# A two-layer image kernel: the remainder's parts of the two output products on separate row halves of the array

## The chip, the cores and the metric

The kernel runs on one core of one Trainium2 chip. A core has TensorE (matmuls; PE in the profile, its weight loads PEld), VectorE (DVE), ScalarE (ACT), GpSimd (POOL) and SyncE (SP, which here only issues DMAs), each with an instruction stream of its own. They meet through semaphores. The metric is the device time of one execution in microseconds (us), lower is better.

## The reference

For a batch of 8 images, x of 192 channels by 64x64 pixels, two layers follow each other:

```
xn  = layernorm over channels(x);  xz = in_proj (384x192) . xn;  xc, z = halves of xz
xc  = silu(conv3x3 depthwise(xc) + b)
y   = sum of four selective scans over 4096 pixels (rows, columns, both directions)
y   = layernorm over channels(y) * out_norm_w + out_norm_b      # LN
y   = y * silu(z)                                               # gate
x1  = x + out_proj (192x192) . y                                # the mix product
theta, phi, g = 96x192 products of x1;  f = softmax(theta^T phi) over 4096 pixels
out = x1 + W (192x96) . (g f^T) + b
```

The 192 channels do not fit the 128 partitions: a tensor over channels is held as a tile of 128 channels and a remainder of 64.

## The kernel before

A loop over the 8 images has three stages, with a barrier of all engines between them. First `project` and the four scans; then the mix stage, which this case is about; then the attention. The 4096 pixels go in 8 chunks (NCH) of 512 (T). Nothing reorders instructions: each engine's stream stands in the order in which its block is written, and waits on semaphores with hand-counted values.

The mix stage is written as `run_mix(eng, step)`: `step(-1, "n")`, `step(0, "np")`, a hardware loop over pairs of steps for chunks 1 to 4, then steps 5 and 6 with "np" and step 7 with "p". In step c, "n" normalizes chunk c+1 and "p" takes chunk c through the products. One step is, by engine (lines of the profile):

- PE: the mean of chunk c+1 (L400, L401 over `pad0` and `yt`), the mix product of chunk c (L629, L630), the variance of chunk c+1 (L400, L401 over `sqa`, `sqb`), two products for the running maximum of attention ("tops", L616), phi (L642, L643), g (L650, L651), two more tops (L616).
- DVE: subtract the mean (`deviate`, L1150, L1151), prepare the remainder of a later chunk (`yt`, L1298), add x to the mix product (`na` L1324, `nb` L1325), two maxima (L1309), then for chunk c+1 four operations: scale `da`, `db` by 1/std (L1335, L1336), shift and gate them into `oa` and `ob` (L1340, L1343); then the low halves `phl`, `gtl` (L1348, L1352), two more maxima (L1309) and a small maximum `mx` (L1359).
- ACT: squares of `da` and `db` (L783, L784), logarithm and exponential for 1/std (L789, L791), copies and splits (L968 to L977).

The variance matmul waits for the squares, they for the deviations, the scaling for 1/std; the mix product waits for `oa` and `ob` (`gated_ready`) and DVE's `na` for the mix product (`mixed`).

In the mix product `wo0` holds the weights for the first 128 input channels and `wo1` those for the remaining 64 in its rows 0 to 63, zeros in rows 64 to 127. Output bank 2 of PSUM takes the first 128 output channels, bank 3 a 128-wide slice whose first 64 rows are the remainder's outputs. `ob` holds the remainder of the input in rows 0 to 63; its rows 64 to 127 are zeroed by GpSimd at the start of each mix stage (`zero_rows`, L1034), so both remainder matmuls run over 128 rows. Tiles alias others in memory, which is why the zeros are set anew for every image. One matmul of these float32 tiles is two records in the trace.

Of the kernel before, what the change touches and what calls it, by code (L numbers as in the profile page):

```python
# [21 lines left out]
ALU = mybir.AluOpType  # L22
# [3 lines left out]
B, C, HH, WW = 8, 192, 64, 64  # L26
L = HH * WW
P = 128
R = C - P
# [21 lines left out]
V_LNW, V_LNB, V_CB, V_DS, V_ONW, V_ONB, V_WB = 0, 2, 4, 6, 14, 16, 18  # L51
# [3 lines left out]
def build(nc, nb, x, vec, w_in, w_x, w_dt, sel, fold, ident, w_out, w_att, gb, w_w, out):  # L55
# [3 lines left out]
    with ctx:  # L59
        def sb(name, shape, dt=F32, where=ctx):  # L60
            return where.enter_context(nc.sbuf_tensor(name, shape, dt))
# [24 lines left out]
        gate = sb("gate", [P, 2, L])  # L86
# [8 lines left out]
        vecs = sb("vecs", [P, NV])  # L95
# [16 lines left out]
        wo1 = sb("wo1", [P, C])  # L112
# [31 lines left out]
        db = sb("db", [R, T], where=lnx)  # L144
        sqa = sb("sqa", [P, T], where=lnx)
        sqb = sb("sqb", [P, T], where=lnx)
# [3 lines left out]
        nb_ = sb("nb", [P, T], where=lnx)  # L150
        oa = sb("oa", [P, T], where=lnx)
        ob = sb("ob", [P, T], where=lnx)
        yt = sb("yt", [P, 2, T], where=lnx)
# [21 lines left out]
        ps = ctx.enter_context(nc.psum_tensor("ps", [P, 8, T], F32))  # L175
# [10 lines left out]
        def barrier(eng, b, n):  # L186
# [6 lines left out]
        S = {n: sem(n) for n in (  # L193

            "pads_set", "rows_zero", "row_one", "xb_zero", "bias_row", "consts_set", "dsum_set", "borders_set", "scan_set", "att_set", "thc_set", "mx_link",

            "x_loaded0", "x_loaded1", "x_free", "mean_ready", "dev_ready", "sq_ready", "var_ready", "rstd_ready",

            "norm_ready", "z_ready", "xc_ready", "zs_ready", "gate_ready", "tap_ready",
            "conv_link", "conv_ready", "tapw_ready", "rem_ready", "rem_free", "cs_ready", "u_ready",  # L200

# [11 lines left out]
        block = ctx.enter_context(nc.Block())  # L213
        LOADS = [(vecs[:, :], vec), (foldw[:, R:P], fold), (eye[:, :], ident), (wo0[:, R:C], w_out[0:P, 0:P]), (wo0[:, 0:R], w_out[0:P, P:C]),
                 (wo1[0:R, R:C], w_out[P:C, 0:P]), (wo1[0:R, 0:R], w_out[P:C, P:C]),
                 (wa0[:, :], w_att[0:P]), (wa1[0:R, :], w_att[P:C]), (wa1[R:R + 1, 2 * O:3 * O], gb), (ww[:, :], w_w), (wdt[0:NX + 1, :].rearrange("p (k n) -> p k n", n=2 * P)[:, 0::2, :], w_dt.rearrange("p (k n) -> p k n", n=2 * P)[:, 0::2, :])]
        wk = w_x.rearrange("p (k n) -> p k n", n=64)
        for w, rows_ in ((wx0, slice(0, P)), (wx1, slice(P, 2 * P))):
            for s, k in enumerate((0, 2)):
                at = s * P  # L220
                LOADS += [(w[:, at:at + NX], w_x[rows_, 64 * k:64 * k + NX]), (w[:, at + R + RANK + NS:at + R + NX], w_x[rows_, 64 * k + RANK + NS:64 * k + NX])]
                for i, kk in enumerate((1, 3)):
                    c_of, m = w_x[rows_, 64 * kk + RANK + NS:64 * kk + NX], at + NX + NS * i
# [168 lines left out]
        def _(pe):  # L392
            mm = pe.matmul
# [23 lines left out]
            with pe.Fori(0, nb) as b:  # L417
# [201 lines left out]
                def step(c, par, which):  # L619
                    i, j = b * NCH + c, b * NCH + (c + 1)  # L620
                    n = (b * 2 + 1) * NCH + (c + 1)
                    q = 1 - par
                    if "n" in which:
                        pe.wait_ge(S["yt_ready"], j + 1)
                        mean_of(0, pad0[:, bass.ds((c + 1) * T, T)], yt[:, q, :], "mean_ready")
                    if "p" in which:
                        pe.wait_ge(S["gated_ready"], i * 2 + 4)
                        for bank, lo, hi in ((2, R, C), (3, 0, P)):
                            mm(ps[:, bank, :], wo0[:, lo:hi], oa[:, :], start=True, stop=False)  # L629
                            m = mm(ps[:, bank, :], wo1[:, lo:hi], ob[:, :], start=False, stop=True)  # L630
                        m.then_inc(S["mixed"], 1)
                    if "n" in which:
                        pe.wait_ge(S["sq_ready"], n * 2 + 2)
                        mean_of(1, sqa[:, :], sqb[:, :], "var_ready")
                    early = "p" in which and not (isinstance(c, int) and c == 0)
                    if early:
                        early_top(c, 0)
                        early_top(c, 1)
                    if "p" in which:
                        pe.wait_ge(S["x1_ready"], i * 2 + 2)  # L640
                        pe.wait_ge(S["phl_ready"], i + 1)
                        mm(ps[:, 4, :], wa0[:, O:O + P], na[:, :], start=True, stop=False)  # L642
                        mm(ps[:, 4, :], wa1[:, O:O + P], nb_[:, :], start=False, stop=True)\  # L643
                            .then_inc(S["phi_ready"], 1)
                        if not early:
                            theta_of(na[:, :], nb_[0:R, :])
                        pe.wait_ge(S["gtl_ready"], i + 1)
                        for t in range(T // P):
                            dst = ps[:, 5, t * P:t * P + O]
                            mm(dst, na[:, t * P:(t + 1) * P], wa0[:, 2 * O:3 * O], start=True, stop=False)  # L650
                            m = mm(dst, nb_[:, t * P:(t + 1) * P], wa1[:, 2 * O:3 * O], start=False, stop=True)  # L651
                        m.then_inc(S["gt_ready"], 1)
                    if early:
                        early_top(c, 2)
                        early_top(c, 3)
                pe.wait_ge(S["rows_zero"], b * 4 + 6)
                pe.wait_ge(S["row_one"], b + 2)
                run_mix(pe, step)
                barrier(pe, b, 1)
# [363 lines left out]
        def _(pool):  # L1023
# [8 lines left out]
            def zero_rows(n, one, tiles):  # L1032
                for t in tiles:
                    pool.memset(t, 0.0).then_inc(S["rows_zero"], 1)  # L1034
                pool.wait_ge(S["rows_zero"], n)
                pool.sem_inc(mark, 1)
                pool.memset(nb_[R:R + 1, :], 1.0).then_inc(S["row_one"], 1)
                pool.wait_ge(S["row_one"], one)
                pool.sem_inc(mark, 1)

            zero_rows(2, 1, (sqb[R:P, :], nb_[R:P, :]))
            with pool.Fori(0, nb) as b:
# [14 lines left out]
                for r, t in enumerate(padi):  # L1057
                    for edge in (t[:, 0:1, :], t[:, PW - 1:PW, :], t[:, 1:PW - 1, 0:1], t[:, 1:PW - 1, PW - 1 - r:PW]):
                        m = pool.memset(edge, 0.0)  # L1059
# [42 lines left out]
                barrier(pool, b, 0)  # L1102


                zero_rows(b * 4 + 6, b + 2, (yt[R:P, :, :], sqb[R:P, :], nb_[R:P, :], ob[R:P, :]))
                pool.memset(xb[R:P, :, :], 0.0).then_inc(S["xb_zero"], 1)
                pool.wait_ge(S["xb_zero"], b + 2)
                pool.sem_inc(mark, 1)
# [9 lines left out]
        def _(dve):  # L1118
            TT, TS, STT = dve.tensor_tensor, dve.tensor_scalar, dve.scalar_tensor_tensor
# [12 lines left out]
            TS(win0[:, :], win0[:, :], vecs[:, V_LNW:V_LNW + 1], None, ALU.mult)  # L1132
            TS(win1[0:R, :], win1[0:R, :], vecs[0:R, V_LNW + 1:V_LNW + 2], None, ALU.mult)

            for name, n in (("x_free", 2), ("fin_ready", 2), ("gated_ready", 2), ("norm_ready", 2), ("gate_ready", 1), ("tap_ready", 1), ("rem_free", 1), ("u_ready", 1),
                            ("xlo_ready", 1), ("dt_ready", 1), ("hc_ready", 3), ("cbc_ready", 4), ("summed", 3), ("y0_added", 1),
                            ("y1_added", 1), ("rows_saved", 16), ("scan_link", 6), ("dbu_ready", 4), ("du_ready", 2), ("dtpre_ready", 1), ("phl_ready", 1), ("gtl_ready", 1),
                            ("top_read", 2), ("pf_ready", 2), ("yraw_ready", 1), ("shift_loaded", 64), ("pv_ready", 2), ("pl_ready", 2),
                            ("yn_ready", 1), ("out_stored", 32)):
                dve.sem_inc(S[name], n)  # L1140
# [25 lines left out]
            with dve.Fori(0, nb) as b:  # L1166
# [144 lines left out]
                def step(c, par, which):  # L1311
                    i, j = b * NCH + c, b * NCH + (c + 1)
                    n = (b * 2 + 1) * NCH + (c + 1)
                    if "n" in which:
                        dve.wait_ge(S["gated_ready"], j * 2 + 2)
                        deviate(n, pad0[:, bass.ds((c + 1) * T, T)], yt[0:R, 1 - par, :])
                        if not isinstance(c, int) or c + 2 < NCH:
                            add_rem(c + 2, par)
# [13 lines left out]
                    if "n" in which:  # L1332
                        dve.wait_ge(S["rstd_ready"], n * 2 + 2)
                        at = j * 2
                        STT(da[:, :], da[:, :], vecs[:, V_ONW:V_ONW + 1], rstd[:, :], ALU.mult, ALU.mult).then_inc(S["mix_link"], 1)  # L1335
                        STT(db[:, :], db[:, :], vecs[0:R, V_ONW + 1:V_ONW + 2], rstd[0:R, :], ALU.mult, ALU.mult)\  # L1336
                            .then_inc(S["mix_link"], 1)
                        sl = bass.ds((c + 1) * T, T)
                        dve.wait_ge(S["mix_link"], at + 1)
                        STT(oa[:, :], da[:, :], vecs[:, V_ONB:V_ONB + 1], gate[:, 0, sl], ALU.add, ALU.mult)\  # L1340
                            .then_inc(S["gated_ready"], 1)
                        dve.wait_ge(S["mix_link"], at + 2)
                        STT(ob[0:R, :], db[:, :], vecs[0:R, V_ONB + 1:V_ONB + 2], gate[0:R, 1, sl], ALU.add, ALU.mult)\  # L1343
                            .then_inc(S["gated_ready"], 1)
                    if "p" in which:
                        sl = bass.ds(c * T, T)
                        dve.wait_ge(S["phh_ready"], i + 1)
# [169 lines left out]
```

## Time and profile before

| | |
|---|---|
| median of 3 runs | 9318.6 us (9313.8 to 9319.06) |
| profiled execution | 9313.63 us, span 9311.9 us |
| PE busy | 8651.9 us, 93% |
| DVE busy | 7376.5 us, 79% |
| ACT busy | 6095.7 us, 65% |
| POOL busy | 3281.4 us, 35% |
| mix product matmuls (L629, L630) | 64 executions of 4 matmuls, 256 records of each line |
| `ob` operation (L1343) | 64 executions, median 736 ns |

Busy time on PE is modelled where matmuls overlap, so a step that shows PE fully busy need not be one that PE sets. A row of the timeline gives start, duration, engine, line, tiles and, in brackets, the idle time of that engine before it and what ended it.

### The profile page before, as it was taken

The page shows a single profiled execution, that of the slowest core. Times are in us where ns is not written, and L with a number is a line of the kernel's source. Part 1 is how long each engine was busy: PE and PEld are TensorE (multiplying, and loading weights), DVE is VectorE, ACT ScalarE, POOL GpSimd, SP SyncE. Part 2 cuts the span into 40 slices and gives each one's busy share as a digit, 9 for nine tenths or more (in the row PEclk, how much of TensorE's full clock was granted, in tenths as well). Part 3 has the DMA queues.
Part 4 walks back from the last instruction along what each step waited for, and adds up shares of the span by engine and source line. Part 5 has one row for each costly group of instructions (what it writes and reads, how often), then busy time and mean ns, then how long its engine had stood idle before and what let it go on. Part 6 is the DMA issues. An engine that isn't in the chain of part 4 may idle for free. (4 is left out here: it accounts for less than half of the span.)

```text
span 9311.9 us, 104022 instructions
## 1 busy us (share of the span) xinstructions
PE 8651.9 (93%) x26448; PEld 4648.7 (50%) x26448; DVE 7376.5 (79%) x8229; ACT 6095.7 (65%) x7440; POOL 3281.4 (35%) x1853
## 2 busy tenths in 40 slices
PE   7899988999989999899988999889998899988999
PEld 2336743367433674336743367333673336733376
DVE  6987769877798777987779876798767987689876
ACT  6765677656776567755677556775567755677566
POOL 2860028600286002860038500385003850038400
PEclk9999999999999999999999999999999999999999
DMA  1320013200132001320023200232002320023200
GB/s 53 111 86 13 10 49 115 82 13 10 56 111 81 11 11 56 115 76 11 11 62 111 76 10 10 66 114 69 10 12 67 111 69 10 12 68 117 65 9 12
DMA packets 286693, 503.21 MB, mean 54 GB/s; under 512 B 142155, under 2 KB 143215, under 8 KB 253431
## 3 DMA queue, kind: packets, MB, share of 16 engines
q1 hardware_dynamic: 286199, 497.81, 17.6%
q8 instruction: 166, 2.72, 0.1%
q14 instruction: 328, 2.69, 0.1%
HBM read 467.99 MB, written 29.47 MB: 53 GB/s over the span
## 5 line engine op out<-in xcount | busy, mean ns | idle before, releaser
L1387 DVE TENSOR_TENSOR pl<-pf,ph 128x1024 fp32r<-128x1024 f32 x1024 | 1254.6, 1225 | 1016.6 <-ACT ph L1013 1008.7
L1241 DVE TENSOR_TENSOR_SCAN h<-ps,h,dbu 128x512 f32<-128x512 f32 x1536 | 1883.8, 1267 | 55.4 <-POOL dbu L1080 30.0
L1080 POOL TENSOR_TENSOR dbu<-bs,du 128x1024 f32<-128x1024 f32 x768 | 1809.3, 2371 | 54.1 <-POOL du L1071 54.1
L1013 ACT ACTIVATE ph<-pf 128x1024 fp32r<-128x1024 f32 x1024 | 1085.3, 1060 | 748.0 <-PE ps L701 747.8
L877 ACT ACTIVATE ps<-dt,negA 128x512 f32<-128x512 f32 x1536 | 1037.9, 687 | 701.8 <-DVE h L1241 701.8
L1007 ACT ACTIVATE pf<-ps 128x1024 f32<-128x1024 f32 x1024 | 1051.4, 1027 | 537.4 <-PE ps L688 537.4
L1371 DVE TENSOR_REDUCE mx<-ps 128x1 f32<-128x512 f32 x1792 | 1168.9, 683 | 77.1 <-PE ps L606 61.9
L1059 POOL MEMSET pad<- 128x66 f32 (+1 forms) x64 | 7.2, 202 | 3179.4 <-DVE fa L1416 3179.2
L1249 DVE TENSOR_TENSOR hc<-h,ps 128x1024 f32<-128x1024 f32 x768 | 937.9, 1221 | 108.0 <-PE ps L487 16.6
L487 PE MATMUL ps<-xhl,selr 128*128 128x512 f32 x1536 | 761.2, 581 | 246.4 <-DVE hc L1249 246.2
L1065 POOL TENSOR_TENSOR dt<-dt,ze 128x1024 f32<-128x1024 f32 x256 | 604.6, 2362 | 1057.7 <-ACT dt L870 1057.1
L686 PE MATMUL ps<-thc,phh 97*128 97x512 f32 x2048 | 847.7, 414 | 6.8 <-ACT thc L990 6.8
L1071 POOL TENSOR_TENSOR du<-dt,u 128x512 f32<-128x512 f32 x512 | 712.7, 1413 | 317.0 <-DVE dt L1231 316.4
L699 PE MATMUL ps<-ph,gth 128*97 128x512 f32 x2048 | 817.7, 399 | 5.5 <-ACT yraw L995 5.5
L687 PE MATMUL ps<-thc,phl 97*128 97x512 f32 x2048 | 816.9, 399 | 0.0
L688 PE MATMUL ps<-thc,phh 97*128 97x512 f32 x2048 | 813.6, 397 | 0.0
L701 PE MATMUL ps<-pl,gth 128*97 128x512 f32 x2048 | 806.8, 394 | 0.0
L700 PE MATMUL ps<-ph,gtl 128*97 128x512 f32 x2048 | 806.4, 394 | 0.0
L487 PEld LDWEIGHTS ps<-xhl,selr 128*128 128x128 f32 x1536 | 245.0, 191 | 905.0 <-DVE hc L1249 732.4
L606 PE MATMUL ps<-phh,thc 96*128 96x512 f32 x1824 | 632.5, 408 | 41.8 <-DVEq L189 18.8
L528 PE MATMUL ps<-hc,eye 128*128 128x512 f32 x1024 | 483.9, 594 | 0.0
L686 PEld LDWEIGHTS ps<-thc,phh 97*128 97x128 f32 x2048 | 389.9, 190 | 174.0 <-issue 78.9
(202 smaller groups left out, 14511.0 us busy)
## 6 DMA issues: line engine op xcount, KB each, us to landing
bs<-rows SPq DMA_DIRECT2D x256, 1024.0 KB, 5.1
bs<-rows SPq DMA_DIRECT2D x512, 256.0 KB, 6.1
xa<-in_x SPq DMA_DIRECT2D x130, 256.0 KB, 2.9
xb<-in_x SPq DMA_DIRECT2D x130, 128.0 KB, 3.0
out<-fa SPq DMA_DIRECT2D x64, 256.0 KB, 2.1
rdb<-rden SPq DMA_DIRECT2D x56, 192.0 KB, 3.4
out<-fa SPq DMA_DIRECT2D x64, 128.0 KB, 2.4
xhl<-ct SPq DMA_DIRECT2D x256, 8.0 KB
```

The lines of the kernel that those rows point to most:

```text
L487: m = mm(flat(ps[:, 4 + e, :]), selr[:, j * P:(j + 1) * P], src, start=True, stop=True)
L686: mm(dst, kk, thc[par][0][:, :], start=True, stop=False)
L687: mm(dst, phl[:, m * P:(m + 1) * P], thc[par][0][:, :], start=False, stop=False)
L699: mm(dst, gth[:, m, :], ph[:, mp % 2, e, :], start=(m == 0), stop=False)
L877: A(ps[:, 2 + e, :], dt[par][:, 0 if j < NS else 1, :], ACT.Exp, scale=negA[:, k * NT + j:k * NT + j + 1]).then_inc(S["dA_ready"], 1)
L1007: A(pf[:, mp % 2, :, :], ps[:, 2 * (mp % 2):2 * (mp % 2) + 2, :], ACT.Exp)\
L1013: A(ph[:, mp % 2, :, :], pf[:, mp % 2, :, :], ACT.Copy).then_inc(S["ph_ready"], 1)
L1080: pool.tensor_tensor(dbu[:, q, :, :], bs[par][:, q, :, :], du[:, r:r + 1, :].to_broadcast([P, 2, T]), ALU.mult).then_inc(S["dbu_ready"], 1)
L1241: dve.tensor_tensor_scan(h[:, j, ::step], ps[:, 2 + e, ::step], dbu[:, q, e, ::step], h[:, j, end:end + 1], ALU.mult, ALU.add)\
L1249: TT(hc[:, q, :, :], h[:, 2 * q:2 * q + 2, :], ps[:, 4:6, :], ALU.mult).then_inc(S["hc_ready"], 1)
L1371: dve.tensor_reduce(mx[:, t, m:m + 1], ps[:, 5 + j % 2, :], AX.X, ALU.max)\
L1387: TT(pl[:, mp % 2, :, :], pf[:, mp % 2, :, :], ph[:, mp % 2, :, :].bitcast(F32), ALU.subtract)\
```

## The change

`wo1` gets a second copy of its weights in rows 64 to 127. DVE computes the gated remainder twice, into rows 0 to 63 and into rows 64 to 127 of `ob`, so `gated_ready` counts three per chunk where it counted two. PE issues the two 128-row matmuls first (banks 2 and 3), then the two remainder matmuls, each over 64 rows: bank 2 from rows 0 to 63 and bank 3 from rows 64 to 127. GpSimd no longer zeroes rows 64 to 127 of `ob`. SyncE loads two more pieces of weights at the start of the program.

```diff
                  (wo1[0:R, R:C], w_out[P:C, 0:P]), (wo1[0:R, 0:R], w_out[P:C, P:C]),
+                 (wo1[R:P, R:C], w_out[P:C, 0:P]), (wo1[R:P, 0:R], w_out[P:C, P:C]),
...
                     if "p" in which:
-                        pe.wait_ge(S["gated_ready"], i * 2 + 4)
-                        for bank, lo, hi in ((2, R, C), (3, 0, P)):
+                        pe.wait_ge(S["gated_ready"], i * 3 + 6)
+                        halves = ((2, R, C, slice(0, R)), (3, 0, P, slice(R, P)))
+                        for bank, lo, hi, _ in halves:
                             mm(ps[:, bank, :], wo0[:, lo:hi], oa[:, :], start=True, stop=False)
-                            m = mm(ps[:, bank, :], wo1[:, lo:hi], ob[:, :], start=False, stop=True)
+                        for bank, lo, hi, at in halves:
+                            m = mm(ps[:, bank, :], wo1[at, lo:hi], ob[at, :], start=False, stop=True)
                         m.then_inc(S["mixed"], 1)
...
-                pe.wait_ge(S["rows_zero"], b * 4 + 6)
+                pe.wait_ge(S["rows_zero"], b * 3 + 5)
...
-                zero_rows(b * 4 + 6, b + 2, (yt[R:P, :, :], sqb[R:P, :], nb_[R:P, :], ob[R:P, :]))
+                zero_rows(b * 3 + 5, b + 2, (yt[R:P, :, :], sqb[R:P, :], nb_[R:P, :]))
...
-                        dve.wait_ge(S["gated_ready"], j * 2 + 2)
+                        dve.wait_ge(S["gated_ready"], j * 3 + 3)
...
-                        STT(ob[0:R, :], db[:, :], vecs[0:R, V_ONB + 1:V_ONB + 2], gate[0:R, 1, sl], ALU.add, ALU.mult)\
-                            .then_inc(S["gated_ready"], 1)
+                        for r in range(2):
+                            STT(ob[r * R:r * R + R, :], db[:, :], vecs[0:R, V_ONB + 1:V_ONB + 2], gate[0:R, 1, sl], ALU.add, ALU.mult)\
+                                .then_inc(S["gated_ready"], 1)
```

On DVE, the second step of the loop before, from the wait for 1/std (L1333) to `gtl`:

```order
L1333 ISA
L1335 SCALAR_TENSOR_TENSOR da<-da,vecs,rstd 128x512
L1336 SCALAR_TENSOR_TENSOR db<-db,vecs,rstd 64x512
L1339 REGISTER_ALU
L1340 REGISTER_ALU
L1340 SCALAR_TENSOR_TENSOR oa<-da,vecs,gate 128x512
L1343 ISA
L1343 SCALAR_TENSOR_TENSOR ob<-db,vecs,gate 64x512
L1348 ISA
L1348 TENSOR_TENSOR phl<-phf,phh 96x512
L1352 ISA
L1352 TENSOR_TENSOR gtl<-ps,gth 128x4x96
```

The same stretch now (line numbers are shifted by three or four):

```order
L1338 SCALAR_TENSOR_TENSOR da<-da,vecs,rstd 128x512
L1339 SCALAR_TENSOR_TENSOR db<-db,vecs,rstd 64x512
L1342 ISA
L1343 REGISTER_ALU
L1343 SCALAR_TENSOR_TENSOR oa<-da,vecs,gate 128x512
L1345 REGISTER_ALU
L1347 ISA
L1347 SCALAR_TENSOR_TENSOR ob<-db,vecs,gate 64x512 x2
L1352 ISA
L1352 TENSOR_TENSOR phl<-phf,phh 96x512
L1356 ISA
L1356 TENSOR_TENSOR gtl<-ps,gth 128x4x96
```

The second `ob` operation stands between the first and `phl`, and with it everything that DVE does until the next `deviate` moves one operation back.

On PE, the same step before, from the mean of chunk c+1 to its variance:

```order
L400 MATMUL ps<-pad,avg 128x512
L401 MATMUL ps<-yt,avg 128x512
L627 ISA
L629 MATMUL ps<-oa,wo 128x512
L630 MATMUL ps<-ob,wo 128x512
L629 MATMUL ps<-oa,wo 128x512
L630 MATMUL ps<-ob,wo 128x512
L633 ISA
L400 MATMUL ps<-sqa,avg 128x512
```

And now:

```order
L401 MATMUL ps<-pad,avg 128x512
L402 MATMUL ps<-yt,avg 128x512
L628 ISA
L631 MATMUL ps<-oa,wo 128x512 x2
L633 MATMUL ps<-ob,wo 128x512 x2
L636 ISA
L401 MATMUL ps<-sqa,avg 128x512
```

The number of matmuls is unchanged. The two of the remainder now stand side by side, over different rows, directly ahead of the variance.

## Rows read from the trace of the kernel before

**Rows 1.** Windows, busy us by engine, granted clock: stage start, one loop step.
```profile
640.00:655.00 15.00, 10.52 (x13) 3.96 (x14) 5.30 (x8) 2.47 (x4) 8.58 (x6) 0.59 0.11 35
...
684.00:696.00 12.00, 11.79 (x43) 6.42 (x42) 10.01 (x16) 5.36 (x10) 0.00 (x0) 1.00 0.11 33
```

**Rows 2.** Timeline, one loop step: start, duration, engine, line, tiles, [idle before].
```profile
684.28 1.29 DVE L1309 TENSOR_REDUCE mx<-ps 128x1 f32<-128x512 f32 x2 [0.51 <-PE ps L616]
...
687.47 0.74 DVE L1343 SCALAR_TENSOR_TENSOR ob<-db,vecs,gate 64x512 f32<-64x512 f32 x1
...
688.13 0.68 DVE L1348 TENSOR_TENSOR phl<-phf,phh 96x512 f32 x1
...
690.01 1.02 PE L629 MATMUL ps<-oa,wo 128*128 128x512 f32 x2
...
690.55 0.17 DVE L1359 TENSOR_TENSOR mx<-mx 128x4 f32<-128x4 f32 x1
...
691.30 0.69 DVE L1150 TENSOR_TENSOR da<-pad,ps 128x512 f32<-128x512 f32 x1 [0.58 <-issue]
...
692.59 1.02 PE L630 MATMUL ps<-ob,wo 128*128 128x512 f32 x2
...
693.15 0.61 ACT L784 ACTIVATE sqb<-db 64x512 f32<-64x512 f32 x1
...
693.82 1.12 PE L400 MATMUL ps<-sqa,avg 128*128 128x512 f32 x2 [0.21 <-ACT sqb L784]
...
696.08 1.29 DVE L1309 TENSOR_REDUCE mx<-ps 128x1 f32<-128x512 f32 x2 [0.91 <-PE ps L616]
```

**Rows 3.** Timeline, the step after it.
```profile
702.68 0.69 DVE L1150 TENSOR_TENSOR da<-pad,ps 128x512 f32<-128x512 f32 x1 [0.17 <-issue]
...
704.53 0.61 ACT L784 ACTIVATE sqb<-db 64x512 f32<-64x512 f32 x1
...
705.23 1.09 PE L400 MATMUL ps<-sqa,avg 128*128 128x512 f32 x2
```

**Rows 4.** Timeline, start of the mix stage of the first image.
```profile
638.63 0.52 POOL L1034 MEMSET nb<- 64x512 f32 x1
639.10 0.52 POOL L1034 MEMSET ob<- 64x512 f32 x1
...
640.35 2.08 PE L400 MATMUL ps<-pad,avg 128*128 128x512 f32 x2 [3.89 <-POOL nb L1037]
```

**Rows 5.** Timeline, mix product of chunk 0 and variance of chunk 2.
```profile
654.67 1.12 PE L629 MATMUL ps<-oa,wo 128*128 128x512 f32 x2 [1.58 <-DVE ob L1343]
...
656.58 0.61 ACT L784 ACTIVATE sqb<-db 64x512 f32<-64x512 f32 x1
...
669.98 0.61 ACT L784 ACTIVATE sqb<-db 64x512 f32<-64x512 f32 x1
...
670.75 1.02 PE L400 MATMUL ps<-sqa,avg 128*128 128x512 f32 x2
```

**Rows 6.** Timeline, 64-row matmuls (64*96) between 128-row ones.
```profile
661.73 1.02 PE L598 MATMUL ps<-na,wa 128*96 128x512 f32 x2
...
662.68 1.10 PE L599 MATMUL ps<-nb,wa 64*96 64x512 f32 x2
...
663.71 0.46 PE L650 MATMUL ps<-wa,na 128*128 128x96 f32 x2
```

**Rows 7.** Timeline, variance of chunk 7 and mix product of chunk 7.
```profile
727.10 0.61 ACT L784 ACTIVATE sqb<-db 64x512 f32<-64x512 f32 x1
...
728.00 1.02 PE L400 MATMUL ps<-sqa,avg 128*128 128x512 f32 x2
...
734.23 1.13 PE L629 MATMUL ps<-oa,wo 128*128 128x512 f32 x2
...
737.96 0.69 DVE L1324 TENSOR_TENSOR na<-ps,xa 128x512 f32<-128x512 f32 x1 [1.32 <-PE ps L630]
```

**Rows 8.** Timeline, weight loads at the start of the program.
```profile
6.26 2.17 SPq L297 DMA_DIRECT2D wo<-in_w_out  x4
```

More of the change, by code:

```diff
@@ L1133, in _ @@
             TS(win1[0:R, :], win1[0:R, :], vecs[0:R, V_LNW + 1:V_LNW + 2], None, ALU.mult)
-            for name, n in (("x_free", 2), ("fin_ready", 2), ("gated_ready", 2), ("norm_ready", 2), ("gate_ready", 1), ("tap_ready", 1), ("rem_free", 1), ("u_ready", 1),
+            for name, n in (("x_free", 2), ("fin_ready", 2), ("gated_ready", 3), ("norm_ready", 2), ("gate_ready", 1), ("tap_ready", 1), ("rem_free", 1), ("u_ready", 1),
                             ("xlo_ready", 1), ("dt_ready", 1), ("hc_ready", 3), ("cbc_ready", 4), ("summed", 3), ("y0_added", 1),
```

## The prediction

> **What bounds the kernel now.** The page's busy shares come first: PE 93%, DVE 79%. They are averages over three stages and the change touches only the mix stage, so the windows come next. In one step of that stage PE is busy 11.79 of 12.00 us and DVE 10.01, at full clock [rows 1]. That reads like a PE bound. The timeline decides, because PE's busy time is modelled. The reader is to follow one step from variance to variance.
>
> PE starts a matmul of the mix product every 0.86 us (690.01 to 692.59 is three of them), so the four end their stream at 692.59 + 0.86 = 693.45. The variance matmul starts at 693.82, on the squares of `db`, which end at 693.15 + 0.61 = 693.76 [rows 2]. So PE waits 0.37 us, and the squares set the start. The squares follow `deviate`, 691.30 to variance being 2.52 us. `deviate` follows DVE's own stream: from the first maxima at 684.28 to `mx` at 690.55 DVE has no idle time (the row of `deviate` shows the first, 0.58 us of issue at the loop's edge, where the loop branches) [rows 2]. The first maxima wait for the tops, which stand on PE behind the variance: 693.82 to 696.08, 2.26 us. So there is a ring: variance, tops, DVE's stretch up to `deviate` (691.30 - 684.28 = 7.02 us at the loop's edge; 702.68 - 696.08 = 6.60 inside it), squares, variance. Inside the loop: 2.26 + 6.60 + 2.51 (702.68 to the squares' end at 704.53 + 0.61 = 705.14, plus the 0.06 us hand-over seen at 693.76 to 693.82, rounded together) = 11.37 us, against 705.23 - 693.82 = 11.41 measured [rows 2, 3]. The ring explains the period. In that step the mix product's stream is free at about the same time (PE's row at 705.23 shows no idle), so PE is second by 0.03 us, not far behind.
>
> **The change, part by part.** All times are for one image; the profiled execution has 8, and I sum against its 9313.63 us (span 9311.9 and 1.7 around it). The median of the runs is 5.0 us above that.
>
> DVE's second `ob`. Each 64x512 operation of this kind holds DVE from 687.47 to 688.13, 0.66 us [rows 2]. It comes after the scaling and ahead of `phl`, `gtl`, two maxima, `mx` and `deviate`, all of them in the ring. Nothing of that stretch waits, so nothing absorbs it. It issues 8 times per image, in steps -1 to 6. That the output now lies on rows 64 to 127 no row shows for this operation; I take the same 0.66.
>
> PE's mix product. Before, 4 x 0.86 = 3.44 us. Two matmuls on separate row halves could run side by side; no row of the trace has such a pair, so I bound the saving s. At best both remainder matmuls take the time of one: 0.86, less the change from 128-row to 64-row work. The rows for that are L598 to L599, 0.95 us where the stream gives 0.86, so 0.09, call it 0.10; and back, L599 to L650, 1.03, so 0.17 [rows 6]. Best case s = 0.76. At worst nothing overlaps and both switches are paid: s = -0.26. I take s = 0.33: each float32 matmul is two records, issued first-first-second-second, and if they start in order, only the second half of the one (0.43) can lie beside the first half of the other, less 0.10. That is between the ends, and is my choice.
>
> TensorE: Matmul & The Clock Gate (Part 3, the mechanism) in the Trainium skill says that matmuls in distinct row groups start about 4 ns apart, though in program order; taken for the whole pair it would give the best case, s = 0.76 less a hair, and the sum would be 2.2 us per image by the working below. TensorEngine Tiling (Key Properties) in the Trainium skill says against this that a change of tiling mode drains the engine; the trace agrees, with the 0.09 and 0.17 us just read.
>
> Where s counts. Inside the loop it counts nothing: the mix product's end is followed by the wait for the squares, which comes later than before. What was hidden behind 3.44 us of matmuls becomes PE idle time. It counts at the two edges, where the mix product itself is on the path.
>
> Now the shift of each point against before:
> - Stage start. PE's first mean waits for GpSimd's zeroing; one 64x512 memset fewer, 639.10 - 638.63 = 0.47 us [rows 4]: -0.47.
> - Mix product of chunk 0. It waits for `ob` (1.58 us idle), so its start moves by +0.66. The variance of chunk 1 follows in PE's stream (the squares end at 657.19, after +0.66 at 657.85; the stream, 654.67 + 3.44 + 0.33, at 658.44): +0.66 - 0.33 = +0.33 [rows 5].
> - Step 0. DVE's extra operation falls before the wait for `gth` and costs nothing. The variance of chunk 2 starts at 670.75 in PE's stream, its squares end at 670.59, 670.64 with hand-over: the 0.33 carried on loses 0.11: +0.22 in all [rows 5].
> - Steps 1 to 4, variances of chunks 3 to 6: +0.66 each by the ring, less the 0.03 by which the squares (705.14 + 0.06) were ahead of PE's stream (705.23) in the step of rows 3, taken for three of the four: 4 x 0.66 - 0.09 = +2.55. 1/std starts from the same variance, and DVE shows no wait for it, so it moves along [rows 2, 3].
> - Step 5, variance of chunk 7: squares ended at 727.71, PE's stream was free at 728.00. With hand-over 0.24 of slack: 0.66 - 0.24 = +0.42 [rows 7].
> - Step 6 and the mix product of chunk 7: it starts at 734.23, as `ob` ends (the row shows no idle, `ob` in the same place of the step takes its 0.74), and now waits for the second: +0.66. Its end releases `na` at 737.96: -0.33. Net +0.33 [rows 7].
> Sum: -0.47 + 0.33 - 0.11 + 2.55 + 0.42 + 0.33 = +3.05 us per image, 24.4 us for eight.
>
> The two weight loads. SyncE took 2.17 us to issue four pieces of `wo` [rows 8], 0.54 each, and every engine waits for the last load: +1.1 us, once.
>
> Total +25.5 us: 9313.6 + 25.5 = 9339 in the profile's terms, 9344 as a median. With s = 0.76 the edges give 0.43 less twice, 2.19 per image, +18.6 in all, 9337. With s = -0.26 the edges give 0.59 more twice, and the variance of chunk 2 is set by the later stream, 0.37 more in place of the squares: 4.6 per image, +38, 9357.
>
> The 64-row copy, the earlier `na` and `nb` in the loop, the register instructions and the semaphore counts I take as nothing: DVE waits for the tops after `nb` in any case (0.51 and 0.91 us [rows 2]), the register instructions lie beside 0.7 us operations. If they lay at the loop's edge, where DVE issues for 0.58 us, they could be worth 0.1 either way, three times an image: 2 us.
>
> **Rivals.**
> First, the PE bound. If the stream of PE and not the ring sets the period (for it: PE is 11.79 of 12.00 busy; the step of rows 3 has no idle before the variance), each np step loses s: 7 steps x 0.33 to 0.76 x 8 = 18 to 43 us, with -0.47 x 8 and +1.1: 9318.6 - 21 to - 45, about 9298 to 9274, faster. Against it: this needs DVE's 0.66 to vanish, and DVE has no idle time between the maxima and `mx`. Chance 7%.
>
> Second, DVE's idle time swallows the operation (0.51, 0.58 and the wait for the mix product in each step [rows 2]) and PE's saving ends in the wait: only the edges remain, -0.47 and at most -0.33 twice: about -9 + 1 us, 9311, no change. Against it: these idle times lie in the ring's other arcs or are issue time. Chance 9%.
>
> Third, the saving s is at its best or above (the pair fully beside each other and the switch hidden), 18.6 us and a little less with a shorter loop edge: 9335, just within what counts as no change. Same mechanism as the forecast, chance 14%.
>
> Fourth, the clock. PE's idle time ahead of the variance grows from 0.37 to about 0.37 + 0.33 + 0.66 = 1.4 us in each step. The granted clock was 0.59 in the stage's first 15 us, where PE had idled 3.89 us [rows 1, 4]; it was 1.00 in the step shown, with 0.37 idle. If the half level (1.2 GHz) lasted one step longer at the start, a step's mix and variance matmuls (6 x 0.86 us) would take 5 us more, of which DVE's ring hides part: 2 to 5 us per image, +16 to +40 more: 9360 to 9384. Against it: PE worked through the 1.58 us wait at 654.67 and ran at 0.86 us per matmul right after. Chance 7%.
>
> **How the numbers follow.** The ring with s between -0.26 and 0.7 has the remaining 63%; it is the likeliest and gives 9344. About 0.2%, 19 us, is what a measurement of this kernel can tell from no change. Slower by more than that: 63 + 7 + a little of the third = 71%. Within: the rest of the third, the second and the lower end of the forecast, 21%. Faster: 8%. The range holds the ring's ends and the third rival: 9331 to 9358; left out are the PE bound, the swallowed operation and the clock.
>
> **What would show it.** Right: the loop's steps take 12.0 us (12.4 at the edge) where they took 11.4 and 11.8; DVE runs gapless from maxima to `mx` with two `ob` rows 0.66 apart; PE shows 1.3 us or more of wait for `sqb` ahead of the variance in each step; the first mean of a stage starts 0.47 us earlier after the barrier. The start-to-start time from the first 128-row matmul of the mix product to the `mixed` release gives s. Wrong would be a step of 11.4 us or less, `deviate` waiting for the mean instead of DVE's stream, a variance matmul without a wait, or a granted clock below 1.00 in the loop's steps.

## The result, and the profile after

| | before | after |
|---|---|---|
| median | 9313.8 us (5 runs, 9305.2 to 9319.1) | 9362.2 us (5 runs, 9344.1 to 9365.7) |
| ratio after/before | | 1.0050, 95% interval 1.0035 to 1.0064 |
| profiled execution | span 9311.9 us, clock 0.978 | span 9342.3 us, clock 0.979 |

The change made the kernel slower, as forecast, but by 48 us in the medians where 25.5 was forecast. The median, 9362, lies 4 us above the range of 9331 to 9358. The profiled execution is 30.4 us longer in span. So there are two questions: whether the 30 us are the ones that were reasoned out, and what the other 18 are.

The timeline of the step of the changed kernel that answers [rows 2, 3] (start, duration, engine, line, tiles, idle before):

```profile
697.81 1.12 PE L401 MATMUL ps<-sqa,avg 128*128 128x512 f32 x2 [1.72 <-ACT sqb L787]
...
700.07 1.29 DVE L1312 TENSOR_REDUCE mx<-ps 128x1 f32<-128x512 f32 x2 [1.13 <-PE ps L617]
...
703.26 1.51 DVE L1347 SCALAR_TENSOR_TENSOR ob<-db,vecs,gate 64x512 f32<-64x512 f32 x2
...
704.80 0.69 DVE L1352 TENSOR_TENSOR phl<-phf,phh 96x512 f32 x1
...
705.79 1.88 PE L631 MATMUL ps<-oa,wo 128*128 128x512 f32 x4
...
707.52 0.69 DVE L1153 TENSOR_TENSOR da<-pad,ps 128x512 f32<-128x512 f32 x1 [0.17 <-issue]
707.60 1.13 PE L633 MATMUL ps<-ob,wo 64*128 64x512 f32 x4
708.13 0.67 DVE L1154 TENSOR_TENSOR db<-yt,ps 64x512 f32<-64x512 f32 x1
708.83 1.03 DVE L1301 TENSOR_TENSOR yt<-gate,ycol 64x512 f32 x1
...
710.03 1.12 PE L401 MATMUL ps<-sqa,avg 128*128 128x512 f32 x2 [1.30 <-ACT sqb L787]
```

From one variance matmul to the next is 12.22 us, against 11.41 in the step of [rows 2] and 11.37 in the one after it. PE now waits 1.30 us for the squares where it showed no wait; 1.72 at the loop's edge, where it showed 0.21. From 700.07 to 707.19 DVE is without idle time, as before. The two `ob` operations take 703.26 to 704.80, 0.77 each and not 0.66. The two 64-row matmuls run side by side as intended: four records of the 128-row product take 1.88 us, four of the 64-row product 1.13 (a record alone takes 0.59 or more), that is 0.75 saved, less 0.09 for the later start (705.79 + 4 x 0.43 = 707.51, against 707.60).

The two edges, answering to [rows 4, 5, 7]:

```profile
639.54 0.52 POOL L1037 MEMSET nb<- 64x512 f32 x1
...
640.79 2.07 PE L401 MATMUL ps<-pad,avg 128*128 128x512 f32 x2 [3.42 <-POOL nb L1040]
...
655.88 3.23 PE L631 MATMUL ps<-oa,wo 128*128 128x512 f32 x4 [2.12 <-DVE ob L1347]
...
741.18 1.98 PE L631 MATMUL ps<-oa,wo 128*128 128x512 f32 x4 [0.58 <-DVE ob L1347]
...
744.27 0.69 DVE L1327 TENSOR_TENSOR na<-ps,xa 128x512 f32<-128x512 f32 x1 [0.56 <-PE ps L633]
```

PE's idle time before the first mean fell from 3.89 to 3.42 us, by the memset's 0.47. The mix product of chunk 7 now waits for `ob` (0.58), and from its start to `na` it is 3.09 us, where it was 3.73: s = 0.64, not 0.33. At 655.88 the four records take 3.23 us in place of 1.88. By the trace's record of the granted clock, the half level at the stage's start had ended 2.8 us earlier. PE waited 2.12 us for the second `ob` (1.58 before), and 0.6 us into the product of chunk 0 the clock fell to its 1.2 GHz level again. Five of the eight images have such a product of chunk 0; in the profile before it is three.

The weight loads, answering to [rows 8]:

```profile
6.26 3.45 SPq L298 DMA_DIRECT2D wo<-in_w_out  x6
...
35.90 0.26 DVE L1124 TENSOR_SCALAR negA<-vecs 128x24 f32<-128x24 f32 x1 [35.90 <-DMA win<-in_w_in]
```

That first DVE operation stood at 34.59 before: +1.31 us.

The account of the 30.4 us, from start times of the mix products. Each part is taken from images with the same clock on both sides: the second row from images whose half level began ahead of the first mean (3 before, 2 now), the others from images at full clock in that part, which agree within 0.05 us. No single image of the changed kernel has all these parts.

| part of an image | forecast | measured |
|---|---|---|
| stage start (memset) | -0.47 | -0.47 |
| first mean to mix product 0 (second `ob`), at the half level | +0.66 | +0.77 (14.32 to 15.09) |
| mix product 0 to 1 (saving, squares of chunk 2) | -0.44 | -0.55 (12.65 to 12.10) |
| mix product 1 to 6 (the ring's steps) | +2.55 | +3.29 (57.25 to 60.54) |
| mix product 6 to 7 | +1.08 | +1.39 (9.63 to 11.02) |
| mix product 7 to `na` (saving) | -0.33 | -0.65 (3.74 to 3.09) |
| sum | +3.05 | +3.78 |

Eight times 3.78 and the loads make 31.5 us, against 30.4. That the whole comes so close is in part luck. By stage, the eight mix stages (first mean to last `na`) took 816.3 us against 782.0, 34.3 more, of which the table accounts for 8 x 4.25 = 34.0. The projection and scan stages took 6.8 us less: 3.8 of that is the memset, which lies ahead of the first mean, and the rest goes with 27 us less time at the half level there in this execution. The attention stages took 1.6 more, and the start 1.3.

### The profile page after: what moved, and what is told of

The parts are those of the page before. It is cut to its first block and busy times, and to the rows that moved or that the text cites. A ratio compares the mean times of both kernels' runs of the same rounds, so it can differ in the third digit from the quotient of the medians.

```text
span 9342.3 us, 104128 instructions
## 1 busy us (share of the span) xinstructions
PE 8612.3 (92%) x26448; PEld 4615.3 (49%) x26448; DVE 7424.7 (79%) x8293; ACT 6097.6 (65%) x7440; POOL 3275.4 (35%) x1845
```

## The experiments

Each, E12 apart, is timed in alternation with the kernel before on the same chip, 5 rounds. Code cuts show only the lines that matter. "Steps" are starts of successive mix products inside the loop, and at its edge in brackets; before they are 11.38 (11.79). "Clock" is the median over the runs of the mean granted clock.

| | us | ratio to before, 95% | steps | clock |
|---|---|---|---|---|
| before, in the four sessions | 9308.9, 9314.7, 9315.4, 9306.6 | | 11.38 (11.79) | 0.978 |
| E1 change again | 9365.9 | 1.0063 (1.0049 to 1.0077) | 12.22 (12.64) | 0.974 |
| E2 second op, rows 0-63 | 9364.2 | 1.0058 (1.0044 to 1.0072) | 11.99 (12.41) | 0.975 |
| E3 second op, rows 64-127 | 9353.7 | 1.0048 (1.0034 to 1.0061) | 12.22 (12.64) | 0.979 |
| E4 PE side only | 9309.7 | 1.0000 (0.9991 to 1.0009) | 11.38 (11.78) | 0.976 |
| E5 copy by ACT | 9319.8 | 1.0009 (1.0000 to 1.0018) | 11.38 (11.79) | 0.977 |
| E6 change, PE filler | 9366.9 | 1.0052 (1.0038 to 1.0066) | 12.22 (12.65) | 0.978 |
| E7 deviate moved | 9313.9 | 1.0001 (0.9992 to 1.0010) | 11.31 (11.68) | 0.977 |
| E8 E5 and E7 | 9307.6 | 0.9996 (0.9987 to 1.0005) | 11.30 (11.60) | 0.977 |
| E9 second op, in and out on 64-127 | 9367.6 | 1.0057 (1.0044 to 1.0071) | 12.23 (12.64) | 0.976 |
| E10 E8 and yt late | 9298.3 | 0.9981 (0.9972 to 0.9990) | 10.90 (10.97) | 0.979 |
| E11 change, both moves | 9314.3 | 0.9998 (0.9989 to 1.0007) | 10.99 and 11.54 (11.71) | 0.977 |
| E12 change, one execution | 9362.8 | | 12.22 (12.64) | 0.973 |
| E13 before and loads | 9315.7 | 1.0012 (1.0003 to 1.0021) | 11.38 (11.79) | 0.979 |
| E14 change, no loads | 9359.0 | 1.0056 (1.0043 to 1.0070) | 12.23 (12.64) | 0.976 |

**E1, the change again.** No edit.

> The changed kernel once more. Theory ring-plus-clock: the change costs about 30 us at equal clock, by steps of the mix loop that take 12.2 us (12.6 at the loop's edge) in place of 11.4 (11.8), and what its runs show beyond that goes with a lower mean granted clock of the run: 9344 at clock 0.979, about 9360 at 0.975. Rival, a second slower level that has nothing to do with the clock: times do not follow the clock of the run.

Of the five runs one took 9334.9 us at clock 0.981, and four took 9362.1 to 9367.3 at 0.974. Of the first five, one took 9344.1 at 0.979 and four took 9360.2 to 9365.7 at 0.973 to 0.975. Times follow the clock.

**E2, the extra DVE operation alone, on rows 0 to 63.** An addition to the kernel before.

```diff
+                        STT(ob2[0:R, :], db[:, :], vecs[0:R, V_ONB + 1:V_ONB + 2], gate[0:R, 1, sl], ALU.add, ALU.mult)\
+                            .then_inc(S["gated_ready"], 1)
```

> The kernel before, with a second gated operation on DVE into another tile on rows 0 to 63 (its result is unused), nothing else. Theory ring, and the move to other rows costs 0.11 us on either side: this one has no move, so each operation costs 0.66, loop steps 12.0 us, and +4.9 us per image, +39 us in all. Rival, every second operation of this kind costs 0.77 to 0.88 whatever its rows: loop steps 12.2 us, +50 us. Rival PE bound: loop steps stay at 11.4 us, under +10 us in all.

The steps are 11.99 us: the ring pays 0.6 for an operation of 0.66 to 0.67, as the timeline of this kernel shows. The total came out at +55 us where +39 was expected, at clock 0.975.

```profile
706.28 0.74 DVE L1344 SCALAR_TENSOR_TENSOR ob<-db,vecs,gate 64x512 f32<-64x512 f32 x1
706.95 0.74 DVE L1346 SCALAR_TENSOR_TENSOR ob<-db,vecs,gate 64x512 f32<-64x512 f32 x1
707.61 0.68 DVE L1351 TENSOR_TENSOR phl<-phf,phh 96x512 f32 x1
```

The PE bound is out: PE's work is unchanged here and every step of the ring is longer.

**E3, the DVE side of the change alone.** Against the changed kernel; the two loads are left out too.

```diff
-                        halves = ((2, R, C, slice(0, R)), (3, 0, P, slice(R, P)))
-                        for bank, lo, hi, _ in halves:
+                        for bank, lo, hi in ((2, R, C), (3, 0, P)):
                             mm(ps[:, bank, :], wo0[:, lo:hi], oa[:, :], start=True, stop=False)
-                        for bank, lo, hi, at in halves:
-                            m = mm(ps[:, bank, :], wo1[at, lo:hi], ob[at, :], start=False, stop=True)
+                            m = mm(ps[:, bank, :], wo1[:, lo:hi], ob[:, :], start=False, stop=True)
```

> The DVE and GpSimd side of the change alone: the second operation goes to rows 64 to 127 of ob, PE multiplies 128 rows as before (the weights of those rows are zero). Theory ring with the move: 0.88 us per operation, loop steps 12.2, per image +5.8 less 0.47 for the memset, +43 us in all. If the move costs nothing, 0.66 and +35 us. Rival PE bound: under +5 us.

Steps of 12.22 us, those of the changed kernel to 0.01. The DVE edit alone makes the whole loss in the loop.

**E4, the PE side alone.** Against the kernel before, with the two loads. Rows 64 to 127 of `ob` stay zero, so the remainder's part is left out of bank 3.

```diff
-                        for bank, lo, hi in ((2, R, C), (3, 0, P)):
+                        halves = ((2, R, C, slice(0, R)), (3, 0, P, slice(R, P)))
+                        for bank, lo, hi, _ in halves:
                             mm(ps[:, bank, :], wo0[:, lo:hi], oa[:, :], start=True, stop=False)
-                            m = mm(ps[:, bank, :], wo1[:, lo:hi], ob[:, :], start=False, stop=True)
+                        for bank, lo, hi, at in halves:
+                            m = mm(ps[:, bank, :], wo1[at, lo:hi], ob[at, :], start=False, stop=True)
```

> The PE side of the change alone (with the two loads): the two remainder matmuls on separate row halves, no second ob; rows 64 to 127 of ob hold zeros, so the remainder's part is missing from bank 3. Theory ring: loop steps inside stay at 11.3 to 11.4 us, PE's saved 0.66 us turns into a wait for the squares, only the stage's edges gain: -1.7 us per image, -13 us with the loads. Rival PE bound: every step loses 0.66, loop steps 10.7, -42 us.

The steps are those of before. The pair is faster and the step is not; the wait for the squares takes it:

```profile
690.81 1.13 PE L633 MATMUL ps<-ob,wo 64*128 64x512 f32 x4
...
692.14 0.61 ACT L787 ACTIVATE sqb<-db 64x512 f32<-64x512 f32 x1
...
692.81 1.13 PE L401 MATMUL ps<-sqa,avg 128*128 128x512 f32 x2 [0.87 <-ACT sqb L787]
```

The sum of the eight mix stages (first mean to last `na`) is 13.8 us less than before. Part of that is the clock: between images with the same clock the stage takes 96.2 us against 97.6, which is 1.4 each and 11 in all, from the first product, the last product and 0.16 in step 6. The medians show no gain. This kernel's runs had clock 0.976 against 0.979 beside them, and 3 of those thousandths are worth about 11 us by the slopes below; why its clock was lower is open.

**E5, the second copy by ACT.** Against the kernel before, with the loads and the PE side of the change.

```diff
+                def twin(j):
+                    act.wait_ge(S["gated_ready"], j * 2 + 4)
+                    A(ob[R:P, :], ob[0:R, :], ACT.Copy).then_inc(S["twin_ready"], 1)
-                        pe.wait_ge(S["gated_ready"], i * 2 + 4)
+                        pe.wait_ge(S["twin_ready"], i + 1)
```

> The change with the second copy of the gated remainder made by ACT (a copy of ob's rows 0 to 63, placed behind the gth copy) in place of DVE. Theory ring: the copy is off the ring, loop steps return to 11.4 (11.8 at the edge), edges gain PE's saving and the memset; mix stage 13 to 18 us shorter over eight images than before, whole kernel -13 us at equal clock, 0 to -13 with the clock of the run. Rival, any second copy costs the step (by a longer wait of the mix product): loop steps 12 us and above, +30 us.

The loop's steps return to 11.38. The forecast gain did not come. From mix product 1 to 2 it takes 12.09 in place of 11.30, since there the copy stands on ACT ahead of the theta split (`thf`, `thc`) behind which DVE's `deviate` is queued. From product 6 to 7 it takes 10.37 in place of 9.63: the last product waits 0.73 us for the copy.

**E6, a filler on PE in the changed kernel.** One more 128-row matmul, whose result is overwritten.

```diff
+                        mm(ps[:, 2, :], wo0[:, R:C], oa[:, :], start=True, stop=True)
```

> The changed kernel with one more 128-row matmul per mix product (0.86 us, its result is overwritten), which lies in PE's wait for the squares. Theory ring plus clock: loop steps stay at 12.2 (12.6), the two edges per image cost up to 0.86 each (+14 us), and less idle time on PE keeps the mean clock higher than in the changed kernel (0.977 or more against 0.974), worth about 4 us per 0.001: total 9355 to 9370. Rival PE bound: steps of 13.1 us, +45 us against the changed kernel. Rival, PE's idle time in the mix stage has nothing to do with the run's clock: clock stays 0.974, total 9377.

PE does 0.86 us more per step and the steps stay at 12.22: PE had that much room. The clock was higher, 0.978, which gave about as much back as the filler cost at the edges.

**E7, deviate ahead of the last maxima.** Against the kernel before.

```diff
+                        if not isinstance(c, int) or c + 2 < NCH:
+                            next_deviate(c + 1, 1 - par)
                         if early:
                             early_top(c - 1, 2, 1 + par, 6)
```

> The kernel before, with DVE's deviate of the next chunk moved ahead of the last two maxima and mx (no other edit). Theory ring: the ring loses 1.5 us and more, PE sets the step: 11.3 us everywhere, the 11.8 at the loop's edge gone, -1 us per image, -5 to -12 us in all. Rival, DVE bound by its total work: no change.

The steps take 11.31 us and PE shows no wait anywhere in the loop: now PE is the bound, and it was second by less than 0.1 us. Removing the ring alone is worth nothing measurable; the 5 to 12 us that were expected did not show in the medians.

**E8, E5 and E7 together.**

> E5 and the move of deviate together. Theory ring: with the ring shortened PE sets the step, and now the saving of the tiled pair (about 0.66 us) counts in each: loop steps 10.6 to 10.8 us, mix stage 45 to 55 us shorter than before over eight images, whole kernel about -45 us, 9255 to 9275. Rival, the pair's saving is never on the path: loop steps as in E7.

The forecast failed: the steps take 11.30 and the whole kernel 9307.6 us, no clear difference from before. A further wait had taken the place; PE waits for `nb` ahead of phi, since `na` and `nb` now stand behind the maxima, `mx` and `yt` on DVE:

```profile
L645 PE MATMUL ps<-na,wa x128: 590/592/697, 656.4 to 8828.3; 128*128 128x512 f32 x128
its engine sat idle before it (us, times) until:
  DVE nb L1340: 47.3, 80
```

**E9, second operation read and written on rows 64 to 127.** Shown against E2.

```diff
-                        STT(ob2[0:R, :], db[:, :], vecs[0:R, ...], gate[0:R, 1, sl], ...
+                        STT(ob2[R:P, :], da[R:P, :], vecs[R:P, ...], gate[R:P, 0, sl], ...
```

> As E2 (the kernel before with a second, unused gated operation on DVE), but this one reads and writes rows 64 to 127, so it lies on the upper rows and moves nothing between rows. Theory, the move between row halves costs 0.1 us on either side: 0.66 us per operation and loop steps of 11.98 us, as in E2. Rival, writing the upper rows costs it: 12.2 us, as in E3 and in the changed kernel.

My theory of a price for moving data between row halves fell. Nothing moves here, and the starts are still 0.77 and 0.78 us apart:

```profile
705.71 0.74 DVE L1344 SCALAR_TENSOR_TENSOR ob<-db,vecs,gate 64x512 f32<-64x512 f32 x1
706.48 0.75 DVE L1346 SCALAR_TENSOR_TENSOR ob<-da,vecs,gate 64x512 f32<-64x512 f32 x1
707.26 0.69 DVE L1351 TENSOR_TENSOR phl<-phf,phh 96x512 f32 x1
```

Against E2 that is 0.11 us more on either side. Two readings are left: being on the upper rows costs it, or changing the first row from one operation to the next does. The trace of the kernel before decides. At its start one operation on rows 0 to 127 (L1126) is followed by two on rows 64 to 127 (L1127, L1128) and one that starts at row 0 again (L1130):

```profile
34.94 0.89 DVE L1126 TENSOR_SCALAR skip<-eye,dsum 128x128 f32<-128x128 f32 x1
35.85 0.29 DVE L1127 TENSOR_SCALAR skip<-eye,dsum 64x128 f32<-64x128 f32 x1
36.05 0.22 DVE L1128 TENSOR_SCALAR eye<-eye 64x128 f32<-64x128 f32 x1
36.28 0.18 DVE L1130 TENSOR_SCALAR negA<-negA 128x24 f32<-128x24 f32 x1
```

The two on the same upper rows overlap: L1128 starts 0.08 us before L1127 ends. L1127 and L1130, whose first row differs from that of the operation ahead, start 0.01 to 0.02 after it has ended. The mix loops show the same two cases in every step: `oa` to `ob`, both from row 0, overlap by 0.07, and so do both `ob` of E2; from `ob` to the second `ob` and on to `phl` the next starts 0.03 after the end in the changed kernel, in E3 and in E9. So it is the change of first row between neighbours that costs 0.11, and not where the operation lies; L1127 and L1128 are one pair of neighbours, but they stand so in every trace.

**E10, E8 with yt behind nb.** Shown against E8.

```diff
+                        if not isinstance(c, int) or c + 2 < NCH:
+                            add_rem(c + 2, par)
                         early = not (isinstance(c, int) and c == 0)
```

> E8 with yt moved behind nb on DVE, so that na and nb no longer wait for the maxima, mx and yt. Theory: in E8 PE waits for nb ahead of phi (0.17 to 0.49 us), which is a new ring; without it PE sets the step and the pair's saving counts: loop steps 10.7 to 10.9 us, mix stage 35 us or more shorter than before over eight images, 9270 to 9285. Rival, the saving of the pair is not to be had in the loop at all: steps stay at 11.3.

The steps take 10.85 to 10.97. In E7 PE fills its step of 11.31 without a wait, so a shorter one needs less work on PE, and the pair is the only edit that gives it: 0.34 to 0.46 us of its saving are there once both rings are off. It is the only version clearly faster than before, 0.9981 (0.9972 to 0.9990), and the 17 us are about half of what was expected. From mix product 1 to 2 it keeps E5's 12.09.

```profile
708.48 1.88 PE L631 MATMUL ps<-oa,wo 128*128 128x512 f32 x4
...
710.29 1.13 PE L633 MATMUL ps<-ob,wo 64*128 64x512 f32 x4
...
710.64 0.61 ACT L787 ACTIVATE sqb<-db 64x512 f32<-64x512 f32 x1
...
711.35 1.13 PE L401 MATMUL ps<-sqa,avg 128*128 128x512 f32 x2
```

PE's variance shows no idle time ahead of it in this step; in the changed kernel it was 1.30.

**E11, the change with both moves.** The two edits of E7 and E10 on the changed kernel.

> The changed kernel (second operation on DVE) with both moves of DVE's order, deviate ahead of the last maxima and yt behind nb. Theory ring: the extra operation leaves the ring's surplus, DVE's whole work of about 10.9 us or PE sets the step: 10.9 to 11.3 us, total 9275 to 9305. Rival, DVE's extra 0.88 us is paid in any order: 12.2 us steps, 9345 and above.

The median is 9314.3 us, no difference from before, where the change alone has a ratio of 1.005. The extra operation off the ring costs far less than on it, but the 9275 to 9305 that were expected did not come: the steps of 11.54 and 11.71 are above the 10.9 to 11.3 of the expectation.

**E12, one more profiled execution of the change.**

> The changed kernel, one look. If its clock is 0.974 to 0.975 as in most of its runs, the theory that it differs from a run at 0.979 by half-clock stretches says that the mix steps are again 12.2 us except those that such a stretch falls in, and that total half-clock time is near 480 us in place of 400, so about 20 us longer. If it is 0.979 again: 9344 or less and nothing new.

The clock was 0.973. The same program as the profile after, over its whole span (busy us and records by engine: PE, PEld, DVE, ACT, POOL; then clock, DMA share, GB/s); first the profile after, then this one:

```profile
0.00:9342.00 9342.00, 8612.26 (x26448) 4615.32 (x26448) 7424.68 (x8293) 6097.62 (x7440) 3275.45 (x1845) 0.98 0.18 54
```

```profile
0.00:9361.00 9361.00, 8651.92 (x26448) 4631.79 (x26448) 7425.04 (x8293) 6094.38 (x7440) 3276.87 (x1845) 0.97 0.18 54
```

DVE and ACT worked as long; PE's same records took 40 us more. The mix steps are 12.22 us again, but for two of 14.31 (the first profile has two of 14.30 as well). By the traces' records of the granted clock, time at the half level was 500 us against 397. The mix stages had 110 of these against 89, and took (first mean to last `na`, eight images) 824.6 us against 816.3. An image takes 99.7 to 100.3 us at best, and 103.4 to 104.0 in most images where the half level comes back; that is 4 of 8 images in the first profile, with one more at 101.7, and 7 of 8 here. So 8 of the 19 us lie in the mix stages. The other 11 lie in the projection and scan stages, with 231 us at the half level against 163; the attention stages differ by under 1 us.

The profiles of all versions show where in the mix stage the half level comes back. In the product of chunk 0 it does so in 6 of 32 images of the four kernels with one `ob` (before, E4, E7, E13), and in 69 of 96 of those with a second copy, by DVE or by ACT, for which that product waits. It costs 1.6 to 1.7 us there (from this product to the next 13.74 in place of 12.10 in the changed kernel, 14.35 in place of 12.65 in E2). In the step at the loop's edge it does so in 7 of 32 images of the changed kernel (the profile after, E1, E12, E14), where PE waits 1.72 us for the squares, and in none of the 96 images of the others, where that wait is 1.07 or less, E6 with its filler among them.

**E13 and E14, the loads.** E13 adds the line with the two loads to the kernel before, E14 takes it from the changed one, which leaves the remainder's part out of bank 3.

> The kernel before with the two extra weight loads (rows 64 to 127 of wo1, which meet zeros of ob). Loads cost their issue: +1.3 us, 9310 to 9320. Theory, the lower clock of the changed kernel's runs comes from the loads (a later start of everything): clock 0.974 to 0.975 and 9325 to 9335. Rival, it does not: clock 0.978.

> The changed kernel without the two loads (rows 64 to 127 of wo1 stay zero, so the remainder's part is missing from bank 3). Theory, the loads lower the clock: clock 0.978 and about 9347. Rival, they do not: clock 0.974 and 9360 to 9366, as in E1.

E13 had clock 0.979, as the kernel before beside it: the loads do not lower it. E14's 0.976 and 9359.0 us lie between the two expectations and decide little alone; without the loads the change still costs 52 us. E13 is 9 us above its before in the medians (interval 3 to 20), where 1.3 was expected. The start of its profile shows 1.2 of it and its mix steps are unchanged; I have no cause for the rest.

## Why the prediction was right and wrong

**What bounds the kernel**: right. The ring of variance, maxima, DVE's stretch, `deviate` and squares sets the step. E2 lengthens it with DVE alone, E4 shortens PE's work and leaves the step as it was, and so does E6, which adds to it. The first rival, PE as the bound, and the second, DVE's idle time as cover, are out. That PE was only just second was also right: E7 gains 0.07 us per step and stops at PE.

**DVE's second `ob`**: wrong in size. The step that failed here is "That the output now lies on rows 64 to 127 no row shows for this operation; I take the same 0.66." The second `ob` holds its place for 0.77 and the first one for 0.77 too, in place of 0.66; that is 0.88 more in all, and the step grew by 0.84. The price is for the change of the first row on both sides of it (E9). The kernel before had a row of this kind, though not for this operation: `yt` reads rows 64 to 127, and it started 0.70 us behind `db` in place of 0.61. Over the ring's steps, step 6 and the first product this is 0.74 + 0.31 + 0.11 = 1.16 us per image, 9.3 us in all.

**The saving s**: wrong in size. "if they start in order, only the second half of the one (0.43) can lie beside the first half of the other." The pair overlaps for the most part: its four records start at 0, 0.007, 0.533 and 0.540 us, so the first records of both matmuls run together and so do the second ones. s was 0.64 to 0.66, inside the bounds and near the best case. The Trainium skill (TensorE: Matmul & The Clock Gate, Part 3, the mechanism) says that matmuls in distinct row groups start about 4 ns apart. The trace agrees for the records of one round, 7 ns apart, and not for the pair as a whole, whose second round starts 0.53 us behind the first. The saving counts at the edges only, as argued: another 0.43 us per image, 3.4 in all, which narrows the error.

**Memset and loads**: right, -0.47 each and +1.3 for 1.1.

So in the profiled execution 30.4 us stand against 25.5, the operation's price and the saving partly cancelling. With both at their measured size the sum would be 31.5 us and the median 9350, by the prediction's own terms, and that is inside the range. The sizes alone did not carry the result out of it.

**The clock**: this took the median out of the range, and it is the step that failed. The sum took the clock's price as nothing, by setting the difference of two profiled executions for the difference of medians, and the range left out the rival that had it ("Fourth, the clock ... Chance 7%"). That rival put the price on the stage's start, 2 to 5 us per image if the half level lasted longer there. The mechanism is real in part. What spoke against it, that "PE worked through the 1.58 us wait at 654.67 and ran at 0.86 us per matmul right after", no longer holds where that wait is 2 us and more: the half level comes back in the first mix product of 21 of 32 images of the changed kernel against 6 of 32 with one `ob`, and at the loop's edge in 7 of 32 against none (E12). At 1.6 us each that is about 9 us per execution, an estimate from these counts.

The runs show the whole price. Over 63 runs of the kernel before in the first three sessions the median clock is 0.978, and a run is about 3.6 us longer for each 0.001 less; over 11 runs of the change it is 0.974 and 3.9 us. On these lines at 0.978 the two stand at 9313 and 9349: 36 us apart. The other 12 of the 48 go with a clock that is lower by 0.003 to 0.004. In E12 over half of the price of more time at the half level lies in the projection and scan stages, where the change edits nothing. Which edit brings that part, or whether one does, is not settled. The loads are not it (E13). PE's longer wait in the loop as its cause has E6 for it (0.978 with the wait filled) and E2 and E9 against it, with 0.975 and 0.976 where PE's wait is shorter than in the change; E3, with the same steps, has 0.979.

## What to carry to other kernels

A step in which the matmul engine shows as fully busy can still be set by a ring through two other engines; follow it from one instruction to the next of the same kind, and price first what an edit adds to that ring. Work taken from an engine that is second pays only when every ring above it is shortened (here two moves of order, E10), and a copy made to let two matmuls run side by side belongs on an engine outside the ring. Look in the trace of before for an operation that starts on the rows the new one will use, whatever its kind: its distance to its neighbours shows the price. Keep some per mille of the range for the granted clock, and ask of each wait of the matmul engine that an edit lengthens whether the clock falls behind it.

## What the runs showed of the hardware

- Two float32 matmuls on rows 0 to 63 and 64 to 127, in two banks, took 1.13 us for their four records, where the four records of two 128-row matmuls take 1.88. The second pair of records starts 0.53 us behind the first, not 0.43. The change to 64-row work cost 0.09.
- A DVE operation whose first row differs from that of the operation ahead started 0.01 to 0.03 us after that one's end; with the same first row it started 0.07 to 0.08 before it. For 512 float32 columns that is 0.77 us from start to start in place of 0.66 (E9 against E2), paid on the way to the other rows and on the way back. Reading the other rows is enough: `yt` started 0.70 us behind `db`, `db` 0.61 behind `da` (708.83, 708.13 and 707.52 in the changed kernel). Two neighbours both on rows 64 to 127 overlap like others (L1127, L1128).
- The same program on the same data had 397 and 500 us at the half clock in two executions, and was 18.7 us longer in span with the second.
- With a second copy of the remainder to wait for, the product that opens the mix stage ran at the half level in 69 of 96 images, without one in 6 of 32, for 1.6 to 1.7 us more.
